# Token-side products of a two-layer transformer kernel in plain fp32 instead of three split passes, on one core of a Trainium2

## The chip, the cores and the metric

The kernel runs on one core of one Trainium2 chip. The metric is the device time of one execution in microseconds (us). The kernel before takes 1779.98 us (median of 3 runs, 1777.85 to 1780.35).

## The reference

Two layers work on 32 sequences of 256 tokens, 128 features wide, all in fp32. Each layer normalises x once and adds an attention and a mixture of experts, both computed from the normalised tokens xn. Cut to what matters:

```python
xn = layernorm(x)
# layer 0: linear attention with 16 heads of 8, and 64 experts of width 64
q, k, v = split(xn @ W_qkv); q, k = rope(q), rope(k)
q_feat, k_feat = elu(q * SCALE) + 1, elu(k) + 1
attn = (q_feat @ (k_feat^T v)) / max(q_feat @ sum(k_feat), 1e-6)
scores = sigmoid(xn @ router_w.T)          # best 8 of the 4 best groups of 8
h = silu(xn @ Wg[e]) * (xn @ Wu[e]) * coef[:, e];  moe = sum_e h @ Wd[e] + shared expert
x = x + attn @ W_out + moe
xn = layernorm(x)
# layer 1: top-8 causal attention with a local message path, and 8 experts of width 256, top 2
q, k, v = xn @ Wq + bq, xn @ Wk + bk, xn @ Wv + bv
x = x + [local messages, softmax(top 8 of q k^T) @ v] @ Wo + bo + experts1(xn, softmax(xn @ gate_w.T))
```

## The kernel before, in words

The 8192 tokens go through in 16 chunks of 512, each of four blocks of 128 tokens. Layer 0's experts are done densely: per chunk 33 tiles (32 pairs of experts and the shared expert). Each step of the main loop (`STEPS`, line 56) gives TensorE one tile's products into the banks `ps_gate` and `ps_up` (`first_products`, line 627), ScalarE its silu, VectorE two products (`times_up`, `times_coef`), and TensorE the down product of the tile three steps before into `ps_y` (`last_products`, line 646). After the 528 tiles, layer 1's experts run over gathered blocks of tokens in the same manner.

Everything else (norms, routing, both attentions) is hung between these tiles as small named steps. `ATTENTION0`, `ROUTE0`, `ROUTE1`, `ATTENTION1` (lines 70 to 88) give for each step the tile after which every engine does its part of it; `PROLOGUE` (line 95) orders the steps of chunk 0 that come before the first tile, among them "split" steps, in which ScalarE and GpSimd part an expert's weights into high and low halves. Layer 1's steps for a chunk run under the tiles of the next one. Each engine goes through its own queue in this fixed order and waits on semaphores. The steps share three PSUM banks, `ps_side`; `TAKES` (line 101) names the step that gives a bank free again, and `make_plan` hands the banks round.

Two kinds of matmul occur. `mm3` (line 602) takes operands that lie as a high half (fp32r, a rounded format) and a low half (the rest), and makes three fp32r passes: high by high, low by high, high by low. A matmul on plain fp32 tiles is one instruction of the program and two in the trace (`ps_y`, line 658, is such a one). The tokens of a chunk, transposed, lie as halves in `xnT` (layer 0) and `xnT1` (layer 1); ScalarE writes the high half (step "xT0", line 1312), VectorE the low one ("x_lo0", line 880).

What the change touches:

- `kv0` to `kv3` (line 713): one `mm3` each for a block of 128 tokens, 256 columns, keys in the left half of the bank and values in the right. VectorE multiplies the keys by the rope tables (lines 973 and 977, three instructions a block), then ScalarE copies the values to `v0` (line 1338).
- `logit0` (line 699): four `mm3` of 64 columns, the routing logits.
- `vl0`, `vl1` (line 754): two `mm3` each of 138 columns, layer 1's values, gate logits and key bias.
- `x_lo0` waits for ScalarE's high half; `logit0` and `kv0` wait for `x_lo0` (`read("xT0", ...)`) and for the low half of the weights (`dve_w0`, line 1245).
- SyncE issues the loads at the start (lines 433 to 440), and waits with the first chunk's `coef_kept` (line 466) for the splits of line 1436.

Of the kernel before, what the change touches and what calls it, by code (L numbers as in the profile page):

```python
# [13 lines left out]
P = 128  # L14
# [55 lines left out]
ATTENTION0 = [(0, "kv0"), (1, "kv1"), (2, "kv2"), (3, "kv3"), (4, "k_rope"), (5, "q"), (6, "q_cos"), (6, "q_swap"), (7, "q_sin"), (8, "q_min"),  # L70
# [27 lines left out]
            "split", "kv0", "split", "kv1", "split", "kv2", "split", "kv3", "split", "k_rope", "q", "split", "q_cos", "split", "q_swap", "split", "q_sin", "q_min", "split"]  # L98
EARLY0 = [(1, "feat_exp"), (3, "q_feat"), (4, "k_feat"), (6, "kvsum"), (7, "kvmask"), (8, "num0"), (9, "num1"), (9, "mix0"), (10, "mix1"), (12, "mixT")]

TAKES = {"xT0": "x_lo0", "logit0": "score_exp", "coefT": "coefT", "kv0": "kv0", "kv1": "kv1", "kv2": "kv2", "kv3": "kv3",
# [55 lines left out]
def build_program(nc, x, ffn_w, att0_w, att0_f, att0_c, e_bias, att1_w, att1_f, att1_b, att1_c, common_c, out):  # L157
    ctx = ExitStack()
    with ctx:
# [44 lines left out]
        w0 = sb("w0", [2, 4 * P + EXPERTS0], FP32R)  # L204
# [21 lines left out]
        w1 = sb("w1", [2, 4 * P + EXPERTS1 + 2], FP32R)  # L226
# [79 lines left out]
        common_in, raw0_in, c0_in, w_out_in, bias0_in = (sem(n) for n in ("common_in", "raw0_in", "c0_in", "w_out_in", "bias0_in"))  # L306
# [108 lines left out]
        def sync(eng):  # L415
# [18 lines left out]
            eng.dma_start(raw0, att0_w).then_inc(raw0_in, 16)  # L434
# [166 lines left out]
        def tensor(eng):  # L601
# [84 lines left out]
            def step(what, key):  # L686
# [12 lines left out]
                elif what == "logit0":  # L699
                    eng.wait_ge(*read("xT0", key))  # L700
                    eng.wait_ge(dve_w0, 1)
                    for r in range(ROWS):
                        ins = mm3(ps[:, r * EXPERTS0:(r + 1) * EXPERTS0], row(halves(key), r), w0_part(4 * P, 4 * P + EXPERTS0))
# [125 lines left out]
        def vector(eng):  # L829
# [40 lines left out]
            def step(what, key):  # L870
# [7 lines left out]
                elif what == "x_lo0":  # L878
                    eng.wait_ge(act_xhi[0], c + 1)
                    eng.tensor_tensor(xnT[:, c % 2, 1], side_bank("xT0", c)[:, :], f32(xnT[:, c % 2, 0]), ALU.subtract).then_inc(read("xT0", c)[0])  # L880
                elif what == "x_lo1":
                    eng.wait_ge(act_xhi[1], c + 1)
# [82 lines left out]
                elif what in ("kv0", "kv1", "kv2", "kv3"):  # L965
                    r = int(what[2])
                    half, ps = (r % 2) * P, side_bank(what, c)
                    eng.wait_ge(*done(what, c))
                    if r == 0 and c == 0:
                        eng.wait_ge(c0_in, 16)  # L970
                    elif r == 0:
                        eng.wait_ge(*done("mixT", c - 1))
                    eng.tensor_tensor(kf[:, r * P:(r + 1) * P], ps[:, 0:P], cosk[:, half:half + P], ALU.mult)
                    k_in, sin_in, k_out = (ap.rearrange("p (h t d) -> p h t d", h=HEADS, t=2) for ap in (
                        ps[:, 0:P], sink[:, half:half + P], tmp0[:, r * P:(r + 1) * P]))
                    for t in range(2):
                        ins = eng.tensor_tensor(k_out[:, :, t], k_in[:, :, 1 - t], sin_in[:, :, t], ALU.mult)
# [649 lines left out]
```

## Time and profile before

| | us |
|---|---|
| median of 3 runs | 1779.98 (1777.85 to 1780.35) |
| the profiled execution's own time | 1780.57 |
| its span, first to last instruction | 1778.6 |
| TensorE matmul busy | 1713.6 (96%) |
| TensorE weight load busy | 1216.1 (68%) |
| VectorE busy | 1360.6 (77%) |
| ScalarE busy | 806.6 (45%) |
| GpSimd busy | 611.4 (34%) |

Busy time is the union of an engine's instructions. A matmul's own duration includes time in which the next one already streams, so that what one costs in a full stream is read from the distance between starts, not from its duration. L603, L604 and L605 are the three passes of `mm3`, whoever calls it; the operands tell which product it is.

### The profile page before, as it was taken

The page shows a single profiled execution, that of the slowest core. Times are in us where ns is not written, and L with a number is a line of the kernel's source. Part 1 is how long each engine was busy: PE and PEld are TensorE (multiplying, and loading weights), DVE is VectorE, ACT ScalarE, POOL GpSimd, SP SyncE. Part 2 cuts the span into 40 slices and gives each one's busy share as a digit, 9 for nine tenths or more (in the row PEclk, how much of TensorE's full clock was granted, in tenths as well). Part 3 has the DMA queues.
Part 4 walks back from the last instruction along what each step waited for, and adds up shares of the span by engine and source line. Part 5 has one row for each costly group of instructions (what it writes and reads, how often), then busy time and mean ns, then how long its engine had stood idle before and what let it go on. Part 6 is the DMA issues. An engine that isn't in the chain of part 4 may idle for free.

```text
span 1778.6 us, 25081 instructions
## 1 busy us (share of the span) xinstructions
PE 1713.6 (96%) x7292; PEld 1216.1 (68%) x7292; DVE 1360.6 (77%) x4012; ACT 806.6 (45%) x1439; POOL 611.4 (34%) x656
## 2 busy tenths in 40 slices
PE   3999999999999999999999999999999998999995
PEld 2666777777777777777777777777777775667763
DVE  5667879796969797978787887878787877566557
ACT  4435454545444454545454535453545343554431
POOL 6212132323232323232323232232324143467770
PEclk9999999999999999999999999999999999999998
DMA  7948363736373636363736354554545445577759
GB/s 214 257 121 241 88 171 86 177 82 181 78 175 76 179 84 180 82 183 82 181 85 171 94 152 113 136 129 112 151 93 152 105 97 159 178 235 226 266 187 308
DMA packets 166470, 269.80 MB, mean 152 GB/s; under 512 B 13688, under 2 KB 52344, under 8 KB 166080
## 3 DMA queue, kind: packets, MB, share of 16 engines
q1 hardware_dynamic: 157760, 250.50, 52.8%
q0 software_dynamic: 8576, 17.70, 3.1%
q8 instruction: 61, 1.00, 0.2%
q14 instruction: 73, 0.60, 0.1%
HBM read 202.21 MB, written 65.93 MB: 151 GB/s over the span
## 4 chain that ended last, share of the span: by engine, by line
PE 93%; DVE 2%; DMA 1%; POOL 1%; issue 1%; ACT 1%; SPq 0%; DVEq 0%; POOLq 0%; ACTq 0%
PE ps_y L658 25%; PE ps_up L603 8%; PE ps_gate L605 8%; PE ps_up L605 8%; PE ps_gate L603 8%; PE ps_up L604 8%; PE ps_gate L604 8%; PE ps_y L684 4%; PE ps_side L624 3%; PE ps_side L605 2%; PE ps_side L603 2%; PE ps_side L604 2%; PE ps_side L793 1%; PE ps_side L776 1%; PE ps_side L735 1%
## 5 line engine op out<-in xcount | busy, mean ns | idle before, releaser
L856 DVE TENSOR_TENSOR silu_h<-ps_up,silu_h 128x512 f32<-128x512 f32 x618 | 423.6, 685 | 339.7 <-ACT silu_h L1264 271.1
L1264 ACT ACTIVATE silu_h<-ps_gate 128x512 f32<-128x512 f32 x618 | 368.1, 599 | 553.4 <-PE ps_gate L605 551.1
L658 PE MATMUL ps_y<-silu_h,w_dn 128*128 128x512 f32 x1056 | 540.7, 593 | 0.4 <-ACT yT L1270 0.4
L850 DVE TENSOR_TENSOR silu_h<-coef_b,silu_h 128x512 f32<-128x512 f32 x528 | 386.2, 731 | 12.0 <-DMA coef_b<-coef_kept 9.6
L603 PE MATMUL ps_gate<-xnT,w_gu 128*128 128x512 f32 x528 | 318.6, 603 | 0.2 <-ACT silu_h L1264 0.2
L658 PEld LDWEIGHTS ps_y<-silu_h,w_dn 128*128 128x128 f32 x1056 | 199.1, 189 | 54.7 <-issue 7.7
L603 PE MATMUL ps_up<-xnT,w_gu 128*128 128x512 f32 x528 | 209.4, 397 | 13.2 <-DVE silu_h L856 13.2
L605 PE MATMUL ps_gate<-xnT,w_gu 128*128 128x512 f32 x528 | 209.4, 397 | 0.0
L605 PE MATMUL ps_up<-xnT,w_gu 128*128 128x512 f32 x528 | 209.3, 396 | 0.0
L604 PE MATMUL ps_up<-xnT,w_gu 128*128 128x512 f32 x528 | 209.2, 396 | 0.0
L604 PE MATMUL ps_gate<-xnT,w_gu 128*128 128x512 f32 x528 | 208.0, 394 | 0.0
L1514 POOL DMA_INDIRECT slots_x<-rows,slot_of x120 | 133.8, 1115 | 178.2 <-PE ps_gate L605 152.6
L1520 POOL TENSOR_TENSOR msg<-msg 128x512 f32<-128x512 f32 x48 | 65.7, 1368 | 312.3 <-ACT msg L1400 309.8
L1493 POOL DMA_INDIRECT y_kept<-ys,y_to x148 | 145.3, 982 | 59.7 <-issue 38.3
L603 PEld LDWEIGHTS ps_gate<-xnT,w_gu 128*128 128x128 f32 x528 | 100.1, 190 | 60.9 <-issue 56.2
L604 PEld LDWEIGHTS ps_gate<-xnT,w_gu 128*128 128x128 f32 x528 | 100.4, 190 | 60.1 <-issue 55.8
L603 PEld LDWEIGHTS ps_up<-xnT,w_gu 128*128 128x128 f32 x528 | 99.5, 188 | 37.8 <-DVE silu_h L856 15.0
L604 PEld LDWEIGHTS ps_up<-xnT,w_gu 128*128 128x128 f32 x528 | 99.4, 188 | 24.0
L605 PEld LDWEIGHTS ps_up<-xnT,w_gu 128*128 128x128 f32 x528 | 99.4, 188 | 23.7
L605 PEld LDWEIGHTS ps_gate<-xnT,w_gu 128*128 128x128 f32 x528 | 99.5, 188 | 22.9
L1445 POOL TENSOR_TENSOR rstd<-rstd,minus_half 128x4 f32<-128x4 f32 x32 | 43.5, 1360 | 162.2 <-DVE shift L868 162.2
L684 PE MATMUL ps_y<-silu_h,w_down 128*128 128x512 f32 x180 | 91.6, 592 | 0.8 <-DVE silu_h L850 0.8
(266 smaller groups left out, 2699.3 us busy)
## 6 DMA issues: line engine op xcount, KB each, us to landing
coef_b<-coef_kept SPq DMA_DIRECT2D x256, 512.0 KB, 6.7
slots_x<-empty SPq DMA_DIRECT2D x15, 2080.0 KB, 12.2
w_block<-w_kept SPq DMA_DIRECT2D x45, 512.0 KB, 3.9
xs<-slots_x SPq DMA_DIRECT2D x37, 260.0 KB, 3.7
y_back<-y_kept SPq DMA_DIRECT2D x15, 512.0 KB, 6.0
w_raw<-in_ffn_w SPq DMA_DIRECT2D x49, 128.0 KB, 3.9
w_down<-in_ffn_w SPq DMA_DIRECT2D x45, 128.0 KB, 3.7
xres<-in_x SPq DMA_DIRECT2D x16, 256.0 KB, 3.2
```

What stands on the lines that cost most here:

```text
L603: eng.matmul(dst, w[0], m[0], start=start, stop=False)
L604: eng.matmul(dst, w[1], m[0], start=False, stop=False)
L605: return eng.matmul(dst, w[0], m[1], start=False, stop=stop)
L624: ins = eng.transpose(ps[:, r * P:(r + 1) * P], rows[:, r * P:(r + 1) * P], ident)
L658: eng.matmul(ps_y[:, :], w_dn[:, j], silu_h[:, g % HBUFS], start=j == 0, stop=last).then_inc(pe_down)
L684: eng.matmul(ps_y[:, :], w_down[:, t % BUFS1, f], silu_h[:, g % HBUFS], start=first, stop=last).then_inc(pe_down)
L850: eng.tensor_tensor(silu_h[:, s], coef_b[:, q % COEF_RING, k], silu_h[:, s], ALU.mult).then_inc(dve_h)
L856: eng.tensor_tensor(silu_h[:, s], ps_up[g % 2][:, :], silu_h[:, s], ALU.mult).then_inc(dve_h1)
L1264: eng.activation(silu_h[:, s], ps_gate[g % 2][:, :], ACT.Silu).then_inc(act_silu)
L1493: eng.indirect_dma_start(y_kept, bass.IndirectOffsetOnAxis(y_to[:, c % XPLACES, r:r + 1], 0), ys[:, c % BUFS1, r], None).then_inc(landed[c ...
L1514: eng.indirect_dma_start(slots_x, bass.IndirectOffsetOnAxis(slot_of[:, r, k:k + 1], 0), rows1[:, c % 2, r], None).then_inc(sent[c % 2], 16)
L1520: eng.tensor_tensor(msg[:, 0], msg[:, 0], msg[:, 1 + k % 2], ALU.add).then_inc(pool_heard)
```

## The change

Layer 0's keys, values and routing logits and layer 1's values, gate logits and key bias are computed by plain fp32 matmuls from unsplit tokens and unsplit weights. ScalarE writes a further copy of the transposed tokens, `x_plain` (layer 1 uses `kT`, which it had already); the weights lie in `w_kvr` (loaded by a transfer of their own) and `w_vl`. The keys of the four blocks go into one bank in one step, `keys0`, the values into another, `values0`. VectorE's rope products for the keys become three instructions over 512 tokens, ScalarE's copies of the values one. The queries, the local messages and the experts keep their three passes.

```diff
-ATTENTION0 = [(0, "kv0"), (1, "kv1"), (2, "kv2"), (3, "kv3"), (4, "k_rope"), (5, "q"), ...
+ATTENTION0 = [(1, "keys0"), (2, "values0"), (2, "k_rope"), (5, "q"), ...
...
-            "split", "kv0", "split", "kv1", "split", "kv2", "split", "kv3", "split", "k_rope", "q", ...
+            "split", "keys0", "split", "split", "values0", "split", "split", "k_rope", "q", ...
...
-        w0 = sb("w0", [2, 4 * P + EXPERTS0], FP32R)
+        w0 = sb("w0", [2, 2 * P], FP32R)
+        w_kvr = sb("w_kvr", [2 * P + EXPERTS0])
+        x_plain = sb("x_plain", [CHUNK])
...
             load_x(0)
-            eng.dma_start(raw0, att0_w).then_inc(raw0_in, 16)
+            eng.dma_start(raw0, att0_w[:, 0:2 * P]).then_inc(raw0_in, 16)
+            eng.dma_start(w_kvr[:, :], att0_w[:, 2 * P:]).then_inc(kvr_in, 16)
             eng.dma_start(common[:, :], common_c).then_inc(common_in, 16)
...
                 elif what == "logit0":
-                    eng.wait_ge(*read("xT0", key))
-                    eng.wait_ge(dve_w0, 1)
+                    eng.wait_ge(act_plain, key + 1)
+                    eng.wait_ge(kvr_in, 16)
                     for r in range(ROWS):
-                        ins = mm3(ps[:, r * EXPERTS0:(r + 1) * EXPERTS0], row(halves(key), r), w0_part(4 * P, 4 * P + EXPERTS0))
+                        ins = eng.matmul(ps[:, r * EXPERTS0:(r + 1) * EXPERTS0], x_plain[:, r * P:(r + 1) * P], w_kvr[:, 2 * P:], start=True, stop=True)
...
-                elif what in ("kv0", "kv1", "kv2", "kv3"):
-                    eng.wait_ge(*read("xT0", key))
-                    mm3(ps[:, 0:2 * P], row(halves(key), int(what[2])), w0_part(2 * P, 4 * P)).then_inc(signal)
-                elif what == "q":
+                elif what in ("keys0", "values0"):
+                    part = w_kvr[:, 0:P] if what == "keys0" else w_kvr[:, P:2 * P]
+                    eng.wait_ge(act_plain, key + 1)
+                    eng.wait_ge(kvr_in, 16)
+                    for r in range(ROWS):
+                        ins = eng.matmul(ps[:, r * P:(r + 1) * P], x_plain[:, r * P:(r + 1) * P], part, start=True, stop=True)
+                    ins.then_inc(signal)
+                elif what == "q":
+                    eng.wait_ge(*read("xT0", key))
+                    eng.wait_ge(dve_w0, 1)
...
                 elif what in ("vl0", "vl1"):
-                    eng.wait_ge(*read("xT1", key))
+                    eng.wait_ge(act_keys, key + 1)
                     eng.wait_ge(*read("fold", 0))
                     for i, r in enumerate(pair(s)):
-                        ins = mm3(ps[:, i * wide:(i + 1) * wide], row(halves1(), r), (w1[:, 0, 3 * P:], w1[:, 1, 3 * P:]))
+                        ins = eng.matmul(ps[:, i * wide:(i + 1) * wide], kT[:, r * P:(r + 1) * P], w_vl[:, :], start=True, stop=True)
...
                 elif what == "x_lo0":
-                    eng.wait_ge(act_xhi[0], c + 1)
+                    eng.wait_ge(act_plain, c + 1)
...
-                elif what in ("kv0", "kv1", "kv2", "kv3"):
-                    eng.tensor_tensor(kf[:, r * P:(r + 1) * P], ps[:, 0:P], cosk[:, half:half + P], ALU.mult)
-                    for t in range(2):
-                        ins = eng.tensor_tensor(k_out[:, :, t], k_in[:, :, 1 - t], sin_in[:, :, t], ALU.mult)
+                elif what == "keys0":
+                    eng.tensor_tensor(seqs(kf[:, :]), seqs(side_bank("keys0", c)[:, :]), cosk.unsqueeze(1).to_broadcast([P, SEQS, SEQ]), ALU.mult)
+                    for t in range(2):
+                        ins = eng.tensor_tensor(k_out[:, :, :, t], k_in[:, :, :, 1 - t],
+                                                sin_in[:, :, t].unsqueeze(1).to_broadcast([P, SEQS, SEQ // HEAD, HEAD // 2]), ALU.mult)
...
-                    eng.copy(xnT[:, c % 2, 0], side_bank("xT0", c)[:, :]).then_inc(act_xhi[0])
+                    eng.copy(xnT[:, c % 2, 0], side_bank("xT0", c)[:, :])
+                    if c > 0:
+                        eng.wait_ge(*done("values0", c - 1))
+                    eng.copy(x_plain[:, :], side_bank("xT0", c)[:, :]).then_inc(act_plain)
...
-                elif what in ("kv0", "kv1", "kv2", "kv3"):
-                    r = int(what[2])
-                    eng.wait_ge(dve_kparts, ROWS * c + r + 1)
-                    eng.copy(v0[:, r, 0:P], side_bank(what, c)[:, P:2 * P]).then_inc(read(what, c)[0])
+                elif what == "values0":
+                    eng.wait_ge(*done("values0", c))
+                    if c > 0:
+                        eng.wait_ge(*done("kvsum", c - 1))
+                    eng.copy(v0[:, :, 0:P], side_bank("values0", c)[:, :].rearrange("p (r d) -> p r d", r=ROWS)).then_inc(read("values0", c)[0])
```

The steps also move between the tiles. TensorE, at the start of chunk 1 (`kv0` and `kv1` are the rows with `w,xnT`; `ps_gate` and `ps_up` are a tile's six passes, `ps_y` a down product). Before:

```order
L603 MATMUL ps_side<-w,xnT 128x256
L604 MATMUL ps_side<-w,xnT 128x256
L605 MATMUL ps_side<-w,xnT 128x256
L603 MATMUL ps_gate<-xnT,w_gu 128x512
L604 MATMUL ps_gate<-xnT,w_gu 128x512
L605 MATMUL ps_gate<-xnT,w_gu 128x512
L603 MATMUL ps_up<-xnT,w_gu 128x512
L604 MATMUL ps_up<-xnT,w_gu 128x512
L605 MATMUL ps_up<-xnT,w_gu 128x512
L658 MATMUL ps_y<-silu_h,w_dn 128x512
L603 MATMUL ps_side<-w,xnT 128x256
L604 MATMUL ps_side<-w,xnT 128x256
```

Now, from the down product ahead of `keys0` to `values0` (line 720 makes both):

```order
L660 MATMUL ps_y<-silu_h,w_dn 128x512
L720 MATMUL ps_side<-w_kvr,x_plain 128x128 x4
L608 MATMUL ps_gate<-xnT,w_gu 128x512
L609 MATMUL ps_gate<-xnT,w_gu 128x512
L610 MATMUL ps_gate<-xnT,w_gu 128x512
L608 MATMUL ps_up<-xnT,w_gu 128x512
L609 MATMUL ps_up<-xnT,w_gu 128x512
L610 MATMUL ps_up<-xnT,w_gu 128x512
L654 MATMUL ps_y<-mix_a,w_out 128x512
L660 MATMUL ps_y<-silu_h,w_dn 128x512
L720 MATMUL ps_side<-w_kvr,x_plain 128x128 x4
```

Where a group of three passes stood after each of tiles 0 to 3, four plain matmuls (eight instructions in a trace) stand after tile 1 and again after tile 2.

VectorE at tile 1 of a chunk, before (lines 850 and 856 are the two products of a tile, lines 973 and 977 a block's keys, line 868 the end of layer 1's statistics):

```order
L868 TENSOR_SCALAR shift<-mean_var 128x4
L850 TENSOR_TENSOR silu_h<-coef_b,silu_h 128x512
L856 TENSOR_TENSOR silu_h<-ps_up,silu_h 128x512
L973 TENSOR_TENSOR kf<-ps_side,att_const 128x128
L977 TENSOR_TENSOR tmp<-ps_side,att_const 128x16x4 x2
L850 TENSOR_TENSOR silu_h<-coef_b,silu_h 128x512
```

Now:

```order
L875 TENSOR_SCALAR shift<-mean_var 128x4
L857 TENSOR_TENSOR silu_h<-coef_b,silu_h 128x512
L863 TENSOR_TENSOR silu_h<-ps_up,silu_h 128x512
L978 TENSOR_TENSOR kf<-ps_side,att_const 128x512
L982 TENSOR_TENSOR tmp<-ps_side,att_const 128x64x4 x2
L857 TENSOR_TENSOR silu_h<-coef_b,silu_h 128x512
```

The keys' products of all four blocks now stand together in front of the second product of tile 1, and none stand at tiles 0, 2 and 3.

## Rows read from the trace of the kernel before

**Rows 1.** The page: the chain that ended last, by engine.

```profile
PE 93%; DVE 2%; DMA 1%; POOL 1%; issue 1%; ACT 1%; SPq 0%; DVEq 0%; POOLq 0%; ACTq 0%
```

**Rows 2.** Busy time by stretch: PE, PEld, DVE, ACT, POOL, then clock, DMA.

```profile
0.00:50.00 50.00, 16.17 (x63) 12.89 (x64) 28.73 (x94) 26.11 (x61) 32.88 (x48) 0.95 0.80 222
50.00:1400.00 1350.00, 1347.96 (x5735) 959.62 (x5734) 1091.47 (x3336) 629.04 (x1119) 388.37 (x394) 1.00 0.53 134
```

**Rows 3.** Timeline of TensorE, a tile without steps: start, duration, line, product.

```profile
808.88 1.02 PE L658 MATMUL ps_y<-silu_h,w_dn 128*128 128x512 f32 x2
...
809.97 0.39 PE L604 MATMUL ps_gate<-xnT,w_gu 128*128 128x512 f32 x1
810.20 0.40 PE L605 MATMUL ps_gate<-xnT,w_gu 128*128 128x512 f32 x1
...
811.13 1.02 PE L658 MATMUL ps_y<-silu_h,w_dn 128*128 128x512 f32 x2
```

**Rows 4.** Timeline of TensorE around `kv1`.

```profile
769.83 1.02 PE L658 MATMUL ps_y<-silu_h,w_dn 128*128 128x512 f32 x2
...
771.28 0.40 PE L604 MATMUL ps_gate<-xnT,w_gu 128*128 128x512 f32 x1
```

**Rows 5.** The same around `xT0` (four transposes), then around `logit0` with `xT1`.

```profile
778.97 1.02 PE L658 MATMUL ps_y<-silu_h,w_dn 128*128 128x512 f32 x2
...
780.50 0.39 PE L604 MATMUL ps_gate<-xnT,w_gu 128*128 128x512 f32 x1
...
790.26 1.02 PE L658 MATMUL ps_y<-silu_h,w_dn 128*128 128x512 f32 x2
...
793.10 0.40 PE L604 MATMUL ps_gate<-xnT,w_gu 128*128 128x512 f32 x1
```

**Rows 6.** The same around `vl0` and `vl1`, up to the queries' second pass.

```profile
796.52 1.02 PE L658 MATMUL ps_y<-silu_h,w_dn 128*128 128x512 f32 x2
...
798.95 0.39 PE L604 MATMUL ps_side<-xnT,w 128*128 128x512 f32 x1
```

**Rows 7.** The same around plain fp32 products: `rank`, `kvsum`, `num0`.

```profile
784.61 1.02 PE L658 MATMUL ps_y<-silu_h,w_dn 128*128 128x512 f32 x2
...
786.15 0.39 PE L604 MATMUL ps_side<-xnT,w 128*128 128x512 f32 x1
...
813.38 1.02 PE L658 MATMUL ps_y<-silu_h,w_dn 128*128 128x512 f32 x2
...
815.37 0.39 PE L604 MATMUL ps_gate<-xnT,w_gu 128*128 128x512 f32 x1
...
821.04 1.02 PE L658 MATMUL ps_y<-silu_h,w_dn 128*128 128x512 f32 x2
...
822.61 0.39 PE L604 MATMUL ps_gate<-xnT,w_gu 128*128 128x512 f32 x1
```

**Rows 8.** Groups by line and shape: VectorE's keys. Busy us, mean ns, idle before.

```profile
L977 DVE TENSOR_TENSOR tmp<-ps_side,att_const 128x64 f32<-128x64 f32 x128 | 22.0, 213 | 0.0
...
L973 DVE TENSOR_TENSOR kf<-ps_side,att_const 128x128 f32<-128x128 f32 x64 | 18.1, 283 | 9.2 <-PE ps_side L605 9.0
```

**Rows 9.** Timelines of VectorE and ScalarE, tiles 2 and 6 of a chunk.

```profile
775.54 0.69 DVE L856 TENSOR_TENSOR silu_h<-ps_up,silu_h 128x512 f32<-128x512 f32 x1 [2.64 <-ACT silu_h L1264]
...
784.17 0.60 ACT L1264 ACTIVATE silu_h<-ps_gate 128x512 f32<-128x512 f32 x1 [2.19 <-PE ps_gate L605]
```

**Rows 10.** Timeline of all engines, the first 50 us.

```profile
1.23 0.49 SPq L434 DMA_DIRECT2D silu_h<-in_att_w  x1
...
6.27 0.24 POOL L1525 TENSOR_SCALAR empty<-common 128x4 f32<-128x4 f32 x1 [5.01 <-DMA common<-in_common_c]
...
10.76 0.59 ACT L1312 CAST xnT<-ps_side 128x512 fp32r<-128x512 f32 x1 [0.67 <-PE ps_side L624]
...
14.93 0.39 ACT L1329 ACTIVATE score<-ps_side 128x256 f32<-128x256 f32 x1 [2.67 <-PE ps_side L605]
...
47.78 0.79 PE L603 MATMUL ps_up<-xnT,w_gu 128*128 128x512 f32 x1 [5.47 <-DVE silu_h L856]
```

More of the change, by code:

```diff
@@ L66 @@
 SPLITS = TILES0 + PARTS1
-ATTENTION0 = [(0, "kv0"), (1, "kv1"), (2, "kv2"), (3, "kv3"), (4, "k_rope"), (5, "q"), (6, "q_cos"), (6, "q_swap"), (7, "q_sin"), (8, "q_min"),
+ATTENTION0 = [(1, "keys0"), (2, "values0"), (2, "k_rope"), (5, "q"), (6, "q_cos"), (6, "q_swap"), (7, "q_sin"), (8, "q_min"),
               (12, "feat_exp"), (13, "q_feat"), (14, "k_feat"), (16, "kvsum"), (17, "kvmask"), (19, "num0"), (20, "num1"), (20, "mix0"),
@@ L97 @@
             "split", "gtop", "split", "gstrike", "split", "groups", "split", "top8", "split", "strike", "split", "weigh", "coefT",
-            "split", "kv0", "split", "kv1", "split", "kv2", "split", "kv3", "split", "k_rope", "q", "split", "q_cos", "split", "q_swap", "split", "q_sin", "q_min", "split"]
+            "split", "keys0", "split", "split", "values0", "split", "split", "k_rope", "q", "split", "q_cos", "split", "q_swap", "split", "q_sin", "q_min", "split"]
 EARLY0 = [(1, "feat_exp"), (3, "q_feat"), (4, "k_feat"), (6, "kvsum"), (7, "kvmask"), (8, "num0"), (9, "num1"), (9, "mix0"), (10, "mix1"), (12, "mixT")]
-TAKES = {"xT0": "x_lo0", "logit0": "score_exp", "coefT": "coefT", "kv0": "kv0", "kv1": "kv1", "kv2": "kv2", "kv3": "kv3",
+TAKES = {"xT0": "x_lo0", "logit0": "score_exp", "coefT": "coefT", "keys0": "keys0", "values0": "values0",
          "q": "q_cos", "q_swap": "q_sin", "kvsum": "kvmask", "num0": "mix0", "num1": "mix1", "mixT": "mixT", "yT": "y_add", "fold": "fold_lo",
@@ L305, in build_program @@
         w_in = [sem(f"w_in{n}") for n in range(STAGES_W)]
[L306 removed]
+        common_in, raw0_in, kvr_in, c0_in, w_out_in, bias0_in = (sem(n) for n in ("common_in", "raw0_in", "kvr_in", "c0_in", "w_out_in", "bias0_in"))
         w_dn_in = [sem(f"w_dn_in{n}") for n in range(TILES0 // DOWN_PART)]
@@ L721, in step @@
                     eng.wait_ge(dve_const, 1)
-                    eng.wait_ge(*read("kv3", key))
-                    eng.wait_ge(*read("kv2", key))
+                    eng.wait_ge(*read("values0", key))
                     eng.wait_ge(dve_kfeat, key + 1)
@@ L964, in step @@
                                              wsum0[:, :].unsqueeze(2).to_broadcast([P, ROWS, EXPERTS0]), ALU.mult, ALU.mult).then_inc(coef_rows)
[L965 to L969 removed]
+                elif what == "keys0":
+                    eng.wait_ge(*done("keys0", c))
+                    if c == 0:
                         eng.wait_ge(c0_in, 16)
[L971 removed]
+                    else:
                         eng.wait_ge(*done("mixT", c - 1))
[L973 to L975 removed]
+                    eng.tensor_tensor(seqs(kf[:, :]), seqs(side_bank("keys0", c)[:, :]), cosk.unsqueeze(1).to_broadcast([P, SEQS, SEQ]), ALU.mult)
+                    k_in, k_out = (ap.rearrange("p (s n t d) -> p s n t d", s=SEQS, t=2, d=HEAD // 2) for ap in (side_bank("keys0", c)[:, :], tmp0[:, :]))
+                    sin_in = sink.rearrange("p (n t d) -> p n t d", t=2, d=HEAD // 2)
                     for t in range(2):
[L977 to L978 removed]
+                        ins = eng.tensor_tensor(k_out[:, :, :, t], k_in[:, :, :, 1 - t],
+                                                sin_in[:, :, t].unsqueeze(1).to_broadcast([P, SEQS, SEQ // HEAD, HEAD // 2]), ALU.mult)
+                    ins.then_inc(read("keys0", c)[0])
                 elif what == "q_cos":
@@ L1317, in step @@
                         eng.wait_ge(*done("vl1", c - 1))
-                    eng.copy(xnT1[:, 0], side_bank("xT1", c)[:, :]).then_inc(act_xhi[1])
+                    eng.copy(xnT1[:, 0], side_bank("xT1", c)[:, :]).then_inc(act_xhi1)
                     if c == 0:
@@ L1355, in step @@
                     eng.wait_ge(raw1_in, 16)
-                    eng.copy(w1[:, 0, P:4 * P + EXPERTS1], raw1[:, P:]).then_inc(act_w1)
+                    eng.copy(w1[:, 0, P:], raw1[:, P:3 * P]).then_inc(act_w1)
                 elif what == "fold":
@@ L1448, in step @@
                 elif what == "k_rope":
-                    eng.wait_ge(dve_kparts, ROWS * (c + 1))
+                    eng.wait_ge(*read("keys0", c))
                     eng.tensor_tensor(kf[:, :], kf[:, :], tmp0[:, :], ALU.add).then_inc(pool_krope)
```

27 lines of the change are left out of this document (12 added, 15 removed).

## Prediction

> **What bounds the kernel now.** I read the chain of waits first: TensorE holds 93% of it [rows 1], so the question is what the change adds to or takes from that engine's queue. The busy time by stretch then says where this holds: from 50 to 1400 us TensorE is busy 1347.96 of 1350 us at full granted clock, while VectorE is busy 81% of it and ScalarE 47% [rows 2]. In the first 50 us TensorE works 16 us and waits for the others. So in the steady part a microsecond less in TensorE's queue is a microsecond less of time, and a VectorE or ScalarE instruction counts only if it makes TensorE wait.
>
> Third, the timeline of TensorE gives prices. Durations overlap there, so I take distances between starts. In a tile without steps, from the start of the down product to the start of the gate's second pass is 809.97 - 808.88 = 1.09 us [rows 3]. A step stands inside that distance, and what it costs is the same distance around it, less 1.09.
>
> **TensorE, what goes** (per chunk):
> - `kv1`: 771.28 - 769.83 - 1.09 = 0.36 us [rows 4] for three passes of 256 columns. The four blocks cost 1.44 us.
> - `logit0`: the distance holds `xT1` too. Four transposes cost 780.50 - 778.97 - 1.09 = 0.44, the two steps 793.10 - 790.26 - 1.09 = 1.75, so the twelve passes of 64 columns cost 1.31 us [rows 5].
> - `vl0` and `vl1`, with the queries' first pass standing where a gate's would: 798.95 - 796.52 - 1.09 = 1.34 us for twelve passes of 138 columns [rows 6].
>
> Together 4.09 us. A pass costs 0.11 to 0.12 us at 64, 138 and 256 columns alike, against 0.23 at 512 [rows 3]: below 256 columns something fixed per pass sets the price, not the columns. That is why the change can pay: it trades twelve small passes for eight.
>
> **TensorE, what comes.** Plain fp32 matmuls of such sizes are in the trace already. `kvsum`, four of 129 columns: 815.37 - 813.38 - 1.09 = 0.90, or 0.225 each. `num0`, two of 144 columns: 822.61 - 821.04 - 1.09 = 0.48, or 0.24 each. `rank`, two of 40 columns: 786.15 - 784.61 - 1.09 = 0.45, again 0.225 each [rows 7]. The new ones lie between these: four of 128 columns for the keys, four for the values and four of 64 for the logits at 0.225, so 0.90 us a step; four of 138 at 0.235 to 0.24, so 0.95. Together 3.65 us.
>
> By part: keys and values lose, 1.80 for 1.44 (+0.36); the logits gain 0.41; layer 1's values gain 0.39. The first two occur in 15 steady chunks (chunk 0's lie in the prologue): 15 x (0.36 - 0.41) = -0.8 us. The third occurs in all 16: -6.2 us. **TensorE sum: -7.0 us**. If every new matmul cost 0.24, the 15 x 12 of layer 0 would add 2.7 us and leave -4.3; reading the starts to 0.01 us allows about 0.5 either way.
>
> **The other engines, priced at nothing.** VectorE's keys cost 18.1 + 22.0 = 40.1 us in all, 2.5 us a chunk [rows 8]. From 128 to 512 elements I take the mean of a 512-wide product on this engine, 0.69 [rows 9], and about 0.4 for each of the two swapped products of 256 elements (an estimate between 213 ns at 64 and 690 at 512): 1.5 us, in one piece at tile 1. Behind it stand tile 1's second product, which TensorE wants only at tile 4, and tile 2's first, before which VectorE idles 2.64 us for ScalarE, which has waited for the chunk's last down product [rows 9]. That idle time covers the piece. If it did not, the next thing late would be tile 4's up product.
>
> ScalarE gets the copy `x_plain` at tile 4, 0.59 us like its neighbour [rows 10], and loses about as much on the values (four small copies become one). Behind the copy stands the next silu; two tiles on ScalarE waits 2.19 us for TensorE [rows 9], which covers it. `x_lo0` waits for the copy too, but its product is wanted by `q_swap` two tiles later. On GpSimd `k_rope` moves two tiles earlier. The three banks pass round with the same or larger distance between a bank's reader and its next writer, two or more tiles around `keys0`, `values0`, `yT` and `xT0`, so I see no new wait for a bank.
>
> **The prologue.** The logits no longer wait for `x_lo0`, but for the copy: about 0.1 us earlier. Then eight instructions stand for twelve. From the end of the high half (10.76 + 0.59) to the exponential at 14.93 there are 3.58 us [rows 10]; less 0.7 for `x_lo0` that is 2.9 for twelve passes with their latency, so a third of them is worth up to 0.9. The splits behind the exponential move with it: -1.0. Against it one more transfer is issued ahead of the constants, which costs SyncE 0.49 us, and GpSimd waits for just these constants (5.01 us idle) on the way to the norm [rows 10]: +0.5. Then comes a queue of transfers, splits and a round trip of the coefficients, which ends at 47.78, when TensorE has idled 5.47 us [rows 10]; it needn't pass the gain on. Ends: -1.0 and +0.5; I take -0.3, near the difference of the two and a little short of it.
>
> **Sum:** -7.0 - 0.3 = -7.3 us. The profiled execution took 1780.57, which gives 1773.3; it lies 0.6 above the median of the runs shown, so I forecast **1772.7 us**. About 0.2% (3.6 us, a boundary at 1776.4) is what a measurement of this kernel can tell from no change.
>
> **Rivals.**
> 1. *Columns decide, and it gets slower.* Old and new products have the same number of output columns per chunk, 1832 (4 x 256 + 4 x 64 + 4 x 138, against 8 x 128 + 4 x 64 + 4 x 138). At 512 columns a split pass costs 0.23 us, three 0.70; a plain product costs 2.25 - 6 x 0.23, some 0.86 [rows 3]. Per column that is 1.36 against 1.68 ns. If the small products followed it, layer 0's 1280 columns in 15 chunks and layer 1's 552 in 16 would add 0.32 ns each: +9 us, 1789. It decides where a pass is long enough for its columns to set its price. The rows at 64 and 138 columns speak against it, since 64 cost what 256 do; only the keys and values, at 256, stand near that point. Chance 3%.
>    The Trainium skill (FP8 and Floating Point Precision, "TensorE Precision Notes") counts four passes through the array for a true fp32 product, where the split form here has three, so by passes alone the change would lose. The trace agrees at 512 columns, 0.86 us against four times 0.23, and shows in the small products that the count of passes isn't what they cost.
> 2. *ScalarE's second copy is exposed.* Were the 0.59 us at tile 4 to reach TensorE in each chunk, 15 x 0.59 = 8.9 us would take the whole gain back: 1781.6. It decides if silu's slack at tiles 4 to 6 falls under 0.59; 2.19 are there [rows 9]. The same if VectorE's piece at tile 1 outlasted its cover in part. Chance 8%.
> 3. *The prologue gives more.* The splits run a microsecond earlier, the transfers follow, and TensorE's idle time before 47.78 shrinks, and with it the time at a lower granted clock (0.95 in the mean of the first 50 us [rows 2]): 2 to 3 us more, 1770.5. Chance 8%.
>
> That the change doesn't do what it says is out: TensorE's order has `x_plain` in place of the three passes at each step.
>
> **How the numbers follow.** The forecast has 79%, the rivals 3, 8 and 8, the rest is unforeseen. The forecast's own ends: -7.5 - 1.0 gives 1771.5 (from the median), -4.3 + 0.5 gives 1776.2. Rival 3 widens it below, part of rival 2 above, and the runs' own spread of about a microsecond to both sides: **1769.8 to 1777.2 us**. Faster by over 0.2%: nearly all of the forecast and rival 3, 0.86. Within: rival 2 and the forecast's upper edge, 0.10. Slower: rival 1 and the unforeseen, 0.04.
>
> **What would show it.** Around each of the three kinds of step, TensorE's starts: 1.99 us for the distance at tiles 1 and 2 of a chunk, 2.43 around `logit0` with `xT1` (2.84 before), 2.04 around the values of layer 1 (2.43 before). TensorE's idle time from 50 to 1400 us stays near 2 us. VectorE's busy time falls by about 16 us, with no effect. Wrong would be: idle time of TensorE at tiles 2 to 6 released by silu or by VectorE; new products of over 0.24 us each; or an exponential of the first chunk that starts at 14.4 or later.

## The result, and the profile after

| | us |
|---|---|
| median of 4 runs, changed | 1767.81 (1766.97 to 1771.06) |
| median of 4 runs of before, beside them | 1779.71 (1777.85 to 1780.35) |
| ratio | 0.9939, 95% interval 0.9925 to 0.9953 |
| the profiled execution's own time, changed | 1767.33 |
| its span | 1765.5 (1778.6 before) |

Faster by 11.9 us. The direction was forecast, the size was not: 1772.7 us was expected, and the range ended at 1769.8.

The page of the changed kernel, its busy times and the chain that ended last by engine:

```profile
span 1765.5 us, 24776 instructions
...
PE 1704.1 (97%) x7228; PEld 1208.2 (68%) x7228; DVE 1350.5 (76%) x3866; ACT 809.7 (46%) x1408; POOL 605.0 (34%) x656
...
PE 93%; DVE 2%; DMA 1%; POOL 1%; issue 1%; ACT 1%; SPq 0%; DVEq 0%; POOLq 0%; ACTq 0%
```

The share of TensorE in the chain is what it was [rows 1]. By stretch (PE, PEld, DVE, ACT, POOL, clock, DMA):

```profile
0.00:50.00 50.00, 17.30 (x65) 13.44 (x66) 26.72 (x85) 25.57 (x58) 33.12 (x48) 0.96 0.78 223
50.00:1400.00 1350.00, 1349.86 (x5723) 960.30 (x5723) 1092.17 (x3232) 635.55 (x1097) 383.64 (x398) 1.00 0.53 136
```

TensorE is as full as before [rows 2]: it idles 0.14 us of the 1350, where it idled 2.04, against a forecast that it would stay near 2. So nearly all of the gain is queue that became shorter, and a trace shows it best as a period: from the start of a chunk's `mix_a` product to that of the next. Two such rows lie 13 chunks apart, in the kernel before:

```profile
223.53 0.59 PE L652 MATMUL ps_y<-mix_a,w_out 128*128 128x512 f32 x1
...
1412.86 0.59 PE L652 MATMUL ps_y<-mix_a,w_out 128*128 128x512 f32 x1
```

and in the changed one:

```profile
219.82 0.59 PE L654 MATMUL ps_y<-mix_a,w_out 128*128 128x512 f32 x1
...
1401.27 0.59 PE L654 MATMUL ps_y<-mix_a,w_out 128*128 128x512 f32 x1
```

Before, (1412.86 - 223.53) / 13 = 91.49 us a chunk; now 90.88. The difference of 0.61, some 15 times, is 9.1 of the 11.9 us. The forecast had 0.44 a chunk. Now the steps, read as in the forecast: the distance from a down product to the gate's second pass around a step, less 1.09 us. TensorE around `keys0`, `values0`, `logit0` with `xT1`, and layer 1's values (L767) with the queries (L608 to L610 on `w`):

```profile
761.99 1.02 PE L660 MATMUL ps_y<-silu_h,w_dn 128*128 128x512 f32 x2
762.85 1.05 PE L720 MATMUL ps_side<-w_kvr,x_plain 128*128 128x128 f32 x8
...
763.97 0.39 PE L609 MATMUL ps_gate<-xnT,w_gu 128*128 128x512 f32 x1
...
765.98 1.02 PE L660 MATMUL ps_y<-silu_h,w_dn 128*128 128x512 f32 x2
...
767.97 0.39 PE L609 MATMUL ps_gate<-xnT,w_gu 128*128 128x512 f32 x1
...
783.03 1.02 PE L660 MATMUL ps_y<-silu_h,w_dn 128*128 128x512 f32 x2
783.89 1.00 PE L705 MATMUL ps_side<-w_kvr,x_plain 128*128 128x64 f32 x8
...
785.40 0.39 PE L609 MATMUL ps_gate<-xnT,w_gu 128*128 128x512 f32 x1
...
788.80 1.02 PE L660 MATMUL ps_y<-silu_h,w_dn 128*128 128x512 f32 x2
789.66 1.10 PE L767 MATMUL ps_side<-w_vl,kT 128*128 128x138 f32 x8
790.71 0.50 PE L608 MATMUL ps_side<-xnT,w 128*128 128x512 f32 x1
791.05 0.40 PE L609 MATMUL ps_side<-xnT,w 128*128 128x512 f32 x1
```

| step | distance forecast | distance measured | cost now | cost before |
|---|---|---|---|---|
| `keys0` | 1.99 | 763.97 - 761.99 = 1.98 | 0.89 | 0.72 (half of four `kv`) |
| `values0` | 1.99 | 767.97 - 765.98 = 1.99 | 0.90 | 0.72 |
| `logit0` with `xT1` | 2.43 | 785.40 - 783.03 = 2.37 | 1.28 | 1.75 |
| layer 1's values | 2.04 | 791.05 - 788.80 = 2.25 | 1.16 | 1.34 |

Three rows of four hold to 0.06. The fourth is 0.21 us late, in each chunk. The eight products themselves are not: they start 0.86 us behind the down product as everything does, and L767 stands as one unbroken piece from 789.66. The queries behind them start late. Which engine held them, the rows of TensorE's products don't say, since a product's modelled end (790.76) reaches past 790.71. The weight load's row does:

```profile
790.71 0.19 PEld L608 LDWEIGHTS ps_side<-xnT,w 128*128 128x128 f32 x1 [0.15 <-ACT score L1336]
```

Groups by line and shape, weight loads of the 80 products of this form, in the kernel before (L603) and changed (L608). Over the whole run the load waited 2.3 us for ScalarE's exponential of the routing scores, before not at all:

```profile
L603 PEld LDWEIGHTS ps_side<-xnT,w 128*128 128x128 f32 x80 | 15.4, 192 | 4.1 <-issue 3.8
```

```profile
L608 PEld LDWEIGHTS ps_side<-xnT,w 128*128 128x128 f32 x80 | 15.4, 192 | 6.3 <-issue 3.8 <-ACT score L1336 2.3
```

Why ScalarE: the queries `q1` take the bank of `logit0`, and `score_exp` gives it free in the same tile, 10. ScalarE in that tile, kernel before, then changed:

```profile
796.08 0.60 ACT L1264 ACTIVATE silu_h<-ps_gate 128x512 f32<-128x512 f32 x1 [1.44 <-PE ps_gate L605]
796.70 1.28 ACT L1329 ACT_TABLE_LOAD   x1
797.99 0.38 ACT L1329 ACTIVATE score<-ps_side 128x256 f32<-128x256 f32 x1
```

```profile
788.36 0.60 ACT L1268 ACTIVATE silu_h<-ps_gate 128x512 f32<-128x512 f32 x1 [1.42 <-PE ps_gate L610]
788.98 1.28 ACT L1336 ACT_TABLE_LOAD   x1
790.27 0.38 ACT L1336 ACTIVATE score<-ps_side 128x256 f32<-128x256 f32 x1
```

In the kernel before, the exponential ended at 798.37 and `q1` was due at 798.67, 0.3 us later. Now it ends at 790.65 and `q1` starts at 790.71: it follows ScalarE. The load of the function table is 1.28 us of that. The Trainium skill (ScalarE: Activation LUTs, "What ACT_TABLE_LOAD costs") gives 1283 ns for the load, which this trace shares, and a further 1.38 us of drain at each switch, which it does not: the exponential starts 0.01 us behind the load.

The other engines did what was forecast in the main: VectorE's keys take 11.0 + 11.9 = 22.9 us where they took 40.1 [rows 8], and TensorE waits for no other step of the steady part. VectorE's busy time as a whole falls by 10.1 us only (1360.6 to 1350.5), where about 16 were forecast; since the engine doesn't set the time, that has no effect.

### The profile page after: what moved, and what is told of

Its sections match the earlier page's. It is cut to its first block, busy times and chain, and to the rows that moved or that the text cites. A ratio compares the mean times of both kernels' runs of the same rounds, so it can differ in the third digit from the quotient of the medians.

```text
span 1765.5 us, 24776 instructions
## 1 busy us (share of the span) xinstructions
PE 1704.1 (97%) x7228; PEld 1208.2 (68%) x7228; DVE 1350.5 (76%) x3866; ACT 809.7 (46%) x1408; POOL 605.0 (34%) x656
## 4 chain that ended last, share of the span: by engine, by line
PE 93%; DVE 2%; DMA 1%; POOL 1%; issue 1%; ACT 1%; SPq 0%; DVEq 0%; POOLq 0%; ACTq 0%
PE ps_y L660 25%; PE ps_gate L608 8%; PE ps_gate L609 8%; PE ps_gate L610 8%; PE ps_up L608 8%; PE ps_up L610 8%; PE ps_up L609 8%; PE ps_y L686 4%; PE ps_side L626 3%; PE ps_side L720 2%; PE ps_side L608 1%; PE ps_side L800 1%; PE ps_side L783 1%; PE ps_side L609 1%; PE ps_side L610 1%
## 5 line engine op out<-in xcount | busy, mean ns | idle before, releaser
L608 PE MATMUL ps_gate<-xnT,w_gu 128*128 128x512 f32 x528 | 329.1, 623 | 0.4 <-DVE tmp L992 0.4
L608 PE MATMUL ps_up<-xnT,w_gu 128*128 128x512 f32 x528 | 207.3, 393 | 9.1 <-DVE silu_h L863 9.1
L609 PE MATMUL ps_gate<-xnT,w_gu 128*128 128x512 f32 x528 | 208.6, 395 | 0.0
L610 PE MATMUL ps_gate<-xnT,w_gu 128*128 128x512 f32 x528 | 208.4, 395 | 0.0
L610 PE MATMUL ps_up<-xnT,w_gu 128*128 128x512 f32 x528 | 207.8, 394 | 0.0
L608 PEld LDWEIGHTS ps_gate<-xnT,w_gu 128*128 128x128 f32 x528 | 100.3, 190 | 65.2 <-issue 56.9
L608 PEld LDWEIGHTS ps_up<-xnT,w_gu 128*128 128x128 f32 x528 | 99.4, 188 | 34.6 <-DVE silu_h L863 11.1
L610 PEld LDWEIGHTS ps_gate<-xnT,w_gu 128*128 128x128 f32 x528 | 99.3, 188 | 23.9
L610 PEld LDWEIGHTS ps_up<-xnT,w_gu 128*128 128x128 f32 x528 | 99.4, 188 | 21.9
## 6 DMA issues: line engine op xcount, KB each, us to landing
slots_x<-empty SPq DMA_DIRECT2D x15, 2080.0 KB, 11.9
```

The source lines that it names most:

```text
L608: eng.matmul(dst, w[0], m[0], start=start, stop=False)
L609: eng.matmul(dst, w[1], m[0], start=False, stop=False)
L610: return eng.matmul(dst, w[0], m[1], start=False, stop=stop)
```

## The experiments

**Which part is worth what, and do addresses count?** The unused memory ahead of the experts' weights differs between the kernels: `w_gu` starts at byte 142496 of a partition before and at 142720 after. First the kernel before with the address alone changed, and the changed kernel with the old addresses:

```diff
+        pad_a = sb("pad_a", [54])
         early = ExitStack()
```

> The kernel before with one unused tile of 216 bytes a partition ahead of the overlaid tiles, so that w_gu, w_dn and all behind them lie exactly where they lie in the changed kernel (w_gu at 142720 instead of 142496, 0 instead of 32 above a multiple of 64); program and order are untouched. Theory A (about 5 of the 12 us come from where the tiles lie): about 1774.5 us, the mean of the up products' passes falls from 397 to about 393 ns. Theory B (they come from the changed order of the work on TensorE): 1779.7 within 1.5 us, 397 ns. Theory C (they come from the prologue or from waits): also 1779.7.

> The changed kernel with every tile of the kernel before at its old address: w_kvr and a pad fill the place of w0's lost columns, w_vl and a pad that of w1's, x_plain lies behind everything. Theory A (addresses): about 1773, near the forecast of 1772.7, passes at 397 ns. Theory B (order of the work) and C (prologue, waits): 1767.8 within 1.5 us, 393 ns.

Then each layer's part of the change alone, both at the old addresses. `l1_only` is the kernel before with this edit and its own weights tile; `l0_only` is the changed kernel with the same edit undone:

```diff
-                        ins = mm3(ps[:, i * wide:(i + 1) * wide], row(halves1(), r), (w1[:, 0, 3 * P:], w1[:, 1, 3 * P:]))
+                        ins = eng.matmul(ps[:, i * wide:(i + 1) * wide], kT[:, r * P:(r + 1) * P], w_vl[:, :], start=True, stop=True)
```

> The kernel before with layer 1's values, gate logits and key bias alone as plain fp32 products; w1 keeps its size and w_vl lies behind everything, so all old tiles keep their addresses. The forecast's term is 16 x 0.39 = 6.2 us: 1773.5, and theories A and C agree. Theory B would let the passes fall below 397 ns too, and give up to 1769.

> The changed kernel with layer 1's values back in three passes, and every old tile at its old address: keys, values and routing logits of layer 0 alone in plain fp32. The forecast's terms: 15 x (0.36 - 0.41) = -0.8 us on TensorE and -0.3 in the prologue, 1778.6. Theory A agrees, at 397 ns. Theory C (the prologue gave several us): 1774 to 1775. Theory B: below 1776 with shorter passes.

| kernel | time | ratio to before | period of a chunk |
|---|---|---|---|
| before | 1779.76 (31 runs) | 1 | 91.49 |
| `b_plus216` | 1775.91 | 0.9977 [0.9967, 0.9987] | 91.17 |
| `a_old_addresses` | 1774.16 | 0.9970 [0.9960, 0.9979] | 91.19 |
| `l1_only` | 1777.03 | 0.9985 [0.9976, 0.9995] | 91.30 |
| `l0_only` | 1776.08 | 0.9981 [0.9972, 0.9991] | 91.37 |
| changed | 1767.81 | 0.9939 [0.9925, 0.9953] | 90.88 |

The periods add: layer 0's part is worth 0.12 us a chunk, layer 1's 0.19, the address 0.32, in all 0.63 against 0.61 for the whole. About half of the change's steady gain is not in its instructions. The times say the same less sharply: `l0_only` is 3.7 us below before, `l1_only` 2.7, `b_plus216` 3.9, in all 10.3 of 11.9, and the changed kernel is 6.4 below `a_old_addresses`; each of them is uncertain by 1.7 us or more. The first pass of the experts' up products in the kernel before, then with the 216 bytes (which the allocator rounds to 224, and which move the same pass from line 603 to line 604), groups by line and shape:

```profile
L603 PE MATMUL ps_up<-xnT,w_gu 128*128 128x512 f32 x528 | 209.4, 397 | 13.2 <-DVE silu_h L856 13.2
```

```profile
L604 PE MATMUL ps_up<-xnT,w_gu 128*128 128x512 f32 x528 | 207.8, 394 | 11.7 <-DVE silu_h L857 11.7
```

Nothing in the program differs but addresses, and a product is 3 ns shorter. The tokens `xnT` lie ahead of the unused bytes and stay where they were; the weights move. Measured as the mean distance between starts in a run of such passes, over some 2,000 pairs of each trace, it is 232.5 ns before and 230.4 with the shift; a tile without steps falls from 2.253 to 2.247 us, 33 of which are 0.2 of the 0.32 us; the rest lies in the tiles with steps.

**Which address?** Three more shifts of the kernel before, by `pad_a` of 8, 16 and 24 elements; in `gu32` the 32 bytes stand behind layer 1's own tiles, so that only the experts' weights and what follows them move.

> The kernel before with 32 unused bytes ahead of the overlaid tiles (the expert weights among them): every one of them moves from an odd to an even multiple of 32 bytes, or the other way (keys and queries of layer 1). Theory M (what counts is the address modulo 64 bytes): 512-column split products follow each other after 230.4 ns instead of 232.5, 1775 to 1776.5 us. Rival D (what counts is the distance to other tiles, or a larger modulus): as before, 232.5 ns and 1779.7 us.

> The kernel before with 64 unused bytes there. Theory M: nothing changes against the kernel before: 232.5 ns, 1779.7 +- 1 us. Rival D: something else, as 216 bytes (which the allocator rounds to 224) gave 230.4 ns.

> The kernel before with 32 unused bytes right ahead of the weights of the experts alone, so that layer 1's queries, keys, scores and messages stay where they were. If the weights' address is the whole effect: 230.4 ns and 1775 to 1776.5 us, as with all tiles moved. If layer 1's tiles carried part of it: in between.

> The kernel before with 96 unused bytes ahead of the overlaid tiles. Measured so far, by the experts' weights' address modulo 128 bytes: 0 gave 230.3 ns (offset 224) and 230.7 (kv_halves), 32 gave 232.5, 64 gave 233.1, 96 gave 233.6 ns a product; modulo 64 is refuted. 96 bytes make the remainder 0 again. Theory L: 230.3 to 230.8 ns, a chunk 91.2 us. Rival (it is the distance of 224 bytes or more, not the remainder): 233 ns or more, a chunk over 91.5 us.

| bytes added | address of `w_gu` modulo 128 | distance of passes, ns | period, us |
|---|---|---|---|
| 0 | 32 | 232.5 | 91.49 |
| 32 | 64 | 233.1 | 91.63 |
| 32, weights alone | 64 | 233.1 | 91.63 |
| 64 | 96 | 233.6 | 91.83 |
| 96 | 0 | 231.3 | 91.41 |
| 224 | 0 | 230.4 | 91.17 |

Modulo 64 is refuted: 32 bytes more made it slower, not faster. That layer 1's tiles carry it is refuted too, by the equal rows at 32. The remainder modulo 128 orders the rows, 0 the fastest, but `p96` with remainder 0 reaches only part of it, and its median of 1778.76 (0.9995 [0.9984, 1.0006]) can't be told from before. In tiles without steps `p96` is as fast as the kernel with 224 bytes, 2.248 us against 2.247; what parts them lies in tiles with steps, 10 to 37 ns in each of some sixteen tiles of a chunk. So: the start address of the weights moves these passes by up to 3.2 ns (1.4%), remainder 0 was best in every kernel that had it, and a second influence besides stays open.

A caution: when `p32`, `p64` and `gu32` ran, and `exp9`, `q1_mid`, `b_exp9` and `kv_halves` below, every kernel, the one before included, took some 48 us more (1828.2 and 1827.55 us for before), and nearly all of that lies after 1500 us, in the last phase. `p32` came out at 1.0026 [1.0011, 1.0041], `p64` at 1.0038 [1.0018, 1.0058], `gu32` at 1.0006 [0.9986, 1.0027]. Why that phase was slower stays open. I compare the periods, which it doesn't touch: `b_exp9` has 91.49 there, as before has elsewhere. `p32`, `p64` and `gu32` ran on a chip on which no other kernel was traced, so that the chip could be a rival for the two slower remainders; but their times there, against the kernel before on the same chip, are longer by 2.1, 5.3 and 1.5 us, and 15 times the difference of the periods is 2.1, 5.1 and 2.1.

**The hidden wait.** Two ways to take away what makes `q1` wait, and a control: the exponential one tile earlier (`exp9` from the changed kernel, `b_exp9` from the one before), and `q1_mid`, from the changed kernel, with the queries taken from their old place to between the two pairs of values:

```diff
-(8, "logit0"), (10, "score_exp")
+(8, "logit0"), (9, "score_exp")
...
-(10, "vl0"), (10, "vl1"),
+(10, "vl0"), (10, "q1"), (10, "vl1"),
```

> The changed kernel with ScalarE's exponential of the routing scores one tile earlier (tile 9 of the chunk, not 10). Theory W (the missing gain of layer 1's values is a hidden wait: layer 1's query products sit right behind the eight plain products and take the bank that the exponential reads, which ends some 0.2 us too late because a table load of 1.28 us stands ahead of it): the query's first product starts about 0.03 us behind the last of the values' instead of 0.23 us and the product after it is not late either; 15 chunks x 0.2 us = 3 us less than the changed kernel's 1767.8: 1764.3 to 1765.3 us. Rival V (the eight plain products themselves cost more than their rows show): nothing changes, 1767.8 +- 0.8 us. Rival S (the earlier table load delays the SiLU of tile 8 and through it TensorE): 1769 us or more, with waits of ps_up for silu_h in every chunk.

> The changed kernel with layer 1's query products between its two pairs of values' products, so that the second pair takes the bank of the routing scores, with 0.47 + 0.69 us of products ahead of it in place of 0.94. Theory W: the 0.2 us wait shrinks to about nothing: 1764.5 to 1766 us. Rival V: 1767.8 +- 0.8 us. If ScalarE's copy of the queries, now earlier, pushes something else, the page shows a new wait.

> The kernel before with the exponential one tile earlier, as the control of exp9. Theory W: in the kernel before the 24 split products (2.7 us) covered table load and exponential, so there is nothing to gain: 1779.7 +- 1 us. Rival S: slower. If it gains 3 us as well, then the wait was in the kernel before too, and theory W does not explain the difference between the kernels.

Against before at 1827.55: `exp9` 1813.46 (0.9932 [0.9907, 0.9957]), `q1_mid` 1810.45 (0.9916 [0.9891, 0.9940]), `b_exp9` 1828.65 (1.0003 [0.9987, 1.0019]). The absolute times expected are void, for the reason above, and the intervals are too wide for 3 us. The periods decide, 90.65 in `exp9` and 90.67 in `q1_mid`, 0.23 and 0.21 less than the changed kernel, and 91.49 in `b_exp9`. TensorE and ScalarE in `exp9`, the same tile:

```profile
788.23 1.02 PE L660 MATMUL ps_y<-silu_h,w_dn 128*128 128x512 f32 x2
...
789.95 0.48 PE L608 MATMUL ps_side<-xnT,w 128*128 128x512 f32 x1
790.27 0.39 PE L609 MATMUL ps_side<-xnT,w 128*128 128x512 f32 x1
```

```profile
786.40 1.28 ACT L1336 ACT_TABLE_LOAD   x1
787.69 0.38 ACT L1336 ACTIVATE score<-ps_side 128x256 f32<-128x256 f32 x1
```

The exponential is over at 788.07, and the distance is 790.27 - 788.23 = 2.04 us: exactly the one forecast for a step without a wait. ScalarE's exponential is gone from what the group's weight loads wait for, in `exp9` as in `q1_mid`, and in `l1_only`, where layer 0 is as before, it is there with 2.0 us. Theory W holds, V and S fall. In the kernel before, the same edit gives nothing, so the wait came with the change.

**Keys and values in halves again.** They cost more in plain form, 1.80 for 1.44, by the forecast as by the rows. Undoing them alone:

```diff
-ATTENTION0 = [(1, "keys0"), (2, "values0"), (2, "k_rope"), ...
+ATTENTION0 = [(0, "kv0"), (1, "kv1"), (2, "kv2"), (3, "kv3"), (4, "k_rope"), ...
```

> The changed kernel with layer 0's keys and values as in the kernel before (four steps, three split passes of 256 columns each), logits and layer 1's values plain; its large tiles stay at addresses that are multiples of 64 bytes. Theory T (the terms add): TensorE's part is 4 x 0.36 = 1.44 us in place of 1.80, so 15 x 0.34 = 5 us less, and the stall of chunk 1 (2.3 us, VectorE late behind a coefficient transfer while ScalarE was held by the value copies) comes back: 1764 to 1766 us, period of a chunk 90.5 us. Rival B (two steps in place of four, with one bank each, are what gives the gain beyond the columns): slower than 1767.8 us, 1769 to 1772.

1809.31 against 1827.55, 0.9909 [0.9872, 0.9945], and a period of 90.56, 0.32 less than the changed kernel. Rival B falls: two steps in place of four bring no gain of their own in the steady part.

**Both together.**

> Both edits in one kernel: the changed kernel with keys and values in halves as before (four steps) and the exponential of the scores one tile earlier. The periods of a chunk found so far (start of a chunk's mix product to the next chunk's) are 90.88 us changed, 90.65 with the earlier exponential, 90.56 with keys and values in halves. Theory T (they add): 90.33 to 90.35 us, and against the changed kernel run beside it 15 x 0.54 = 8 us less, minus some 1 us for chunk 1, so 6.5 to 8 us less. Rival: the two share a cause (ScalarE's queue), and the period stays at 90.5 to 90.6.

> The same with unused bytes that put the other tiles TensorE reads (layer 0's and layer 1's projection weights, the plain tokens, layer 1's queries, keys, scores) at multiples of 128 bytes as well; the experts' weights are at such an address in both. Theory L (an operand at a multiple of 128 bytes is read faster): the small split and plain products gain as the experts' did (about 2 ns a product, some 130 of them a chunk: up to 0.2 us a chunk, 3 us in all). Rival: only the large weights, or their place against the tokens, count: same time as kv_exp9 within 1 us.

> The changed kernel unedited, as the anchor for this chip: period of a chunk 90.88 us and ratio 0.9939 to the kernel before if the chip is like the first; on a chip whose last phase (layer 1's experts) is slower in every kernel, the same period and the same difference in microseconds.

Here before took 1780.07 us (13 runs), `after_again` 1768.75 (0.9934 [0.9918, 0.9951]), `kv_exp9` 1761.47 (0.9895 [0.9878, 0.9911]) and `kv_exp9_al` 1761.06 (0.9892 [0.9875, 0.9908]). The rows of `kv_exp9`:

```profile
221.08 0.59 PE L657 MATMUL ps_y<-mix_a,w_out 128*128 128x512 f32 x1
...
1395.45 0.59 PE L657 MATMUL ps_y<-mix_a,w_out 128*128 128x512 f32 x1
```

(1395.45 - 221.08) / 13 = 90.34: the two terms add to 0.01 us. It is 7.3 us faster than the changed kernel and 18.6 faster than before, the best version found. Multiples of 128 bytes for the small operands gave 0.06 us a chunk more (90.28) and no time that can be told apart; the large passes, some 200 a chunk and 230.2 ns against 230.7, can account for all of it. Theory L is not borne out for small products.

**What happens once.** Chunk 1's period is not the steady one. In the kernel before, TensorE waits at its start, as the only long wait between 50 and 1400 us:

```profile
134.53 0.50 PE L603 MATMUL ps_up<-xnT,w_gu 128*128 128x512 f32 x1 [1.67 <-DVE silu_h L856]
```

VectorE had waited for the coefficients just before, and in the changed kernel it waits for them as long. Kernel before, then changed:

```profile
133.19 0.69 DVE L850 TENSOR_TENSOR silu_h<-coef_b,silu_h 128x512 f32<-128x512 f32 x1 [5.06 <-DMA coef_b<-coef_kept]
```

```profile
131.23 0.69 DVE L857 TENSOR_TENSOR silu_h<-coef_b,silu_h 128x512 f32<-128x512 f32 x1 [5.02 <-DMA coef_b<-coef_kept]
```

But in the kernel before ScalarE stood still with the copy of `kv1`'s values at the head of its queue, ahead of `yT` and the next silu. Its rows, kernel before:

```profile
134.97 0.27 ACT L1338 COPY v<-ps_side 128x128 f32<-128x128 f32 x1 [7.50 <-DVE tmp L977]
135.13 0.59 ACT L1270 COPY yT<-ps_y 128x512 f32<-128x512 f32 x1
135.61 0.61 ACT L1264 ACTIVATE silu_h<-ps_gate 128x512 f32<-128x512 f32 x1
```

That copy waited for VectorE's rope; in the changed kernel the values have a bank of their own, their copy waits for TensorE alone, and `yT` and silu go first. Same view, changed kernel:

```profile
131.08 0.59 ACT L1274 COPY yT<-ps_y 128x512 f32<-128x512 f32 x1 [4.88 <-PE ps_y L660]
131.56 0.61 ACT L1268 ACTIVATE silu_h<-ps_gate 128x512 f32<-128x512 f32 x1
132.05 0.59 ACT L1346 COPY v<-ps_side 128x512 f32<-128x512 f32 x1
```

Chunk 1's period, less the kernel's own steady one, is on average 1.7 us over the eight traces with values in halves and no plain logits (0.6 to 2.1), and -0.2 over the six with `keys0` and `values0` (-0.5 to 0.7). In the three kernels with `kv` steps brought back it is 1.0, 1.5 and 3.7. So the two banks are worth some 1.9 us, once, with much scatter, presumably since it hangs on when the coefficients land. That is read from groups of traces; no run changes the two banks alone. The prologue gave less than this scatter: the first `mix_a` product starts at 129.16 us in the changed kernel and 129.93 before, but at 129.75 in `after_again` and from 129.3 to 135.0 in other traces that have the old prologue.

## Why the prediction was wrong

The time fell below the range because the sum has no term for where the tiles lie (4.8 us by the periods) and none for chunk 1 (about 1.9 us). Its largest term, layer 1's values, was twice too big, because the step "I see no new wait for a bank" failed; that hid part of what was missing.

- *The views and the bound*: right. TensorE's queue set the time, and VectorE, ScalarE's second copy and the moved `k_rope` cost nothing.
- *Prices of the new products* (0.225 and 0.235 to 0.24 us, from `kvsum`, `num0` and `rank`): right to 0.01 us a step, in `keys0`, `values0`, and, once its wait is gone, in layer 1's values.
- *Layer 0, "+0.36" and "0.41", 15 x (0.36 - 0.41) = -0.8 us*: the keys and values came as forecast, the logits gained 0.47 (1.75 to 1.28), and the isolated part has 0.12 a chunk, some 1.8 us.
- *Layer 1's values, "0.39 ... in all 16: -6.2 us"*: **the sum's largest term was twice too big.** Measured alone it is 0.19 a chunk, 3.0 us. The step that failed here is "I see no new wait for a bank". I had looked at the banks around the steps whose place in the table moved. Around `vl` and `q1` nothing moved in the table, but the twelve passes removed there were the cover of `score_exp`, which frees `q1`'s bank in the same tile, 0.3 us before it was wanted. Of the 0.39 us taken from ahead of it 0.30 were margin; the rest and a hand-over of 0.06 (790.65 to 790.71) are the 0.15 us in the weight load's row, and the queries' second pass came 0.2 us late. `exp9` and `q1_mid` both gave it back.
- *Missing from the sum: addresses, put at nothing without a reason.* The change shrinks and adds tiles, so what lies behind them moves by 224 bytes, and that is worth 0.32 us a chunk, 4.8 us, 3.9 by the time of `b_plus216`, 6.4 by that of `a_old_addresses`. The forecast has no term for it, and no row of the trace before could price it. At the old addresses the changed kernel takes 1774.16 us, 1.5 from the forecast; that it comes so near is luck in part, since there the missing gains of layer 0 and chunk 1 nearly make up for layer 1's values.
- *Missing as well: chunk 1*, some 1.9 us. The profile had it: the wait of ScalarE for VectorE ahead of each value copy, and a stall there.
- *Prologue, -0.3 us*: the pieces went as worked out, the score's exponential starts at 14.06 (14.93 before [rows 10]), but GpSimd's wait for the constants ended at 6.42, 0.15 later and not 0.5 [rows 10]. TensorE's start is within the scatter, so -0.3 is neither confirmed nor refuted.
- *Rivals*: columns don't decide, 64, 128 and 138 columns cost alike. ScalarE's second copy is hidden. The prologue did not give 2 us; the time was close to that rival's 1770.5 for other reasons.

By term: -1.8 (layer 0), -3.0 (layer 1), -4.8 (addresses), -1.9 (chunk 1) make -11.5 of the -11.9 us measured. That they fit so well is luck in part: in the two profiled executions, 13.1 us apart in their spans, the last chunk of layer 0 alone differs by 0.9 us more than a steady one, and between traces of one program it scatters by as much. Program terms alone, -4.8, were over-estimated at -7.0, and two unpriced ones more than made up for it: the miss of nearly 5 us to the fast side is in the main an error of 2 to the one side and of 7 to the other.

## What to carry to other kernels

Work that is removed was cover for something: ask which bank, buffer or copy the next instruction of that queue needs, when it comes free, and what is left of the margin (here 0.3 us against 0.39 taken away), above all where a step's giver and taker share a tile. Price each kind of product of a change by itself: the plain form paid for 64 and 138 columns in twelve passes and lost at 256 in twelve, and keeping only the paying parts was worth 0.3 us a chunk more. When a change alters the size of tiles, run the old kernel with the new addresses beside it, or a shift of the weights is booked as the gain of the edit.

## What the runs showed of the hardware

- The start address of a weight tile in SBUF changes how fast 512-column split passes follow each other: 230.4 and 231.3 ns where it was a multiple of 128 bytes, 232.5, 233.1 and 233.6 at remainders 32, 64 and 96, same program. The cause, and why two addresses with remainder 0 differ by 0.9 ns, stay open.
- A wait of TensorE for a bank need not show as idle time: the products' modelled ends cover it. In the group's row for weight loads it was 2.3 us in sum, while 0.2 us a chunk, 3 us, went by on TensorE.
- Plain fp32 products of 64, 128 and 138 columns cost nearly the same, 0.84 (1.28 less 0.44 for `xT1`), 0.90 and 0.95 us for four, where twelve split passes cost 1.31 at 64 columns and 1.34 at 138.
